# Another written-out order of the steps for a four-layer graph network kernel on one core

## The chip, the core and the metric

The kernel runs on one core of one Trainium2 chip. The metric is the device time of one execution in microseconds, the median of several runs. The core has five engines with a queue of instructions each: TensorE (PE, its weight loads are listed as PEld), VectorE (DVE), ScalarE (ACT), GpSimd (POOL) and SyncE (SP, which here only issues the DMAs of x and of the result).

## The reference, cut to what matters

x has 32 graphs of 512 nodes with 128 features. Every layer takes the layer norm of x, a relu, and adds the layer's result to x. adj is the same 512 by 512 matrix for all graphs.

```python
h = jnp.maximum(_layernorm(x, axis=-1), 0.0)
x = x + _L0_gnn_ref(h, adj, ...)   # attention whose scores come from pairs of nodes, plus h @ self_weight
h = jnp.maximum(_layernorm(x, axis=-1), 0.0)
x = x + _L1_gnn_ref(h, adj, ...)   # graph attention, layer norm, neighbour sum, two-layer MLP
h = jnp.maximum(_layernorm(x, axis=-1), 0.0)
x = x + _L2_gnn_ref(h, adj, ...)   # graph attention, elu
h = jnp.maximum(_layernorm(x, axis=-1), 0.0)
x = x + _L3_gnn_ref(h, adj, ...)   # two projections and one fixed 512 x 512 mixing matrix
```

## The kernel before

The 32 graphs are worked on in 16 groups of two. A group goes through 57 steps (STEPS, lines 50 to 107): `load` reads its x by two DMAs of 256 KB, `store` writes the result back by two such DMAs, and the steps between compute the four layers. Each step has a part on one to three engines. Ten more steps (PREP, "g" in the tables) make the fixed matrix of the last layer once, at the start.

Six groups are in flight, each in a slot of its own: group n uses the tiles whose name ends in n modulo 6 (X4, Y4, HT4 and so on), so group 14 has X2, group 13 X1, group 12 X0, group 11 X5, group 10 X4 and group 15 X3. The x of groups 0 to 2 is read before the main block, that of groups 3 to 5 by `load` once the preparation is over (`edge["done"]`, line 620), since their tiles lie where the preparation's were, and each later one when the group six before it has been stored.

What order each engine works in is written out by hand in TURNS (lines 120 to 139). There is one string for each engine, with one character for each step: the group (0 to f, g for the preparation) whose next step is done. The steps of one group stay in the order of STEPS. HOMES (line 140) says for each PSUM tile, in PE's order, which of the eight PSUM banks it takes. `walk` (line 280) runs through an engine's list and calls a function for each step. Engines wait for each other by semaphores that count the executions of a step. An engine works strictly in its order: a step whose input is late holds up all that stand behind it.

Lines that the steps below touch: `load` waits for the slot's last store and issues its DMAs on SP (lines 616 to 623). `store` waits on SP until DVE has finished the group's last step agg3, then issues two DMAs (lines 625 to 628). `stat0` on DVE takes eight BATCH_NORM_STATS2 of x (line 1154) as soon as x is loaded. `split0` (lines 1211 to 1222) and `low0` (line 1227) on DVE make the operands of `agg0` on PE (line 695); `cmax0` on DVE is lines 1177 to 1189. `mean2` on POOL is lines 1107 and 1109, `top2` on DVE lines 1268 to 1278, and `agg3` on DVE line 1456, twice for a group.

Of the kernel before, what the change touches and what calls it, by code (L numbers as in the profile page):

```python
# [117 lines left out]
    ("eturn", 4, "pe act dve"),  # L118
]
TURNS = {  # L120
    "pe": ("ggggg0110101020g221001241423030413011003310441051152525330125202312322303320414313055000101101040415"
           "2141541504245540525210132132224264222673676643477266237334323443343446764886786648687675785737835778"
           "584838848854595595959965a6a99a56a6a79799696699679675a56656a777787a78776b6ba8bab8a6a7b78aba88b8979b88"
           "abacb8b89cdb9cbadab8cdcd89d9899acaa9ac99daea9cecaacdecebccedbdcdeebd9bddde9e9bebbebceecbeffbfaffbcbd"
           "fcfadafffdffdfcfcccecdcedccfddfeddedffbdeeefeffefebfecedfcffbdcedfefef"),
    "act": ("gg01012g02g10124430301120401310505110301541022130321202303125103301200101411425025443010254524025113"
           "4512345232624246372753644622372343437346446388668747866537573653586877448854788759955956aa9686a69579"
           "876969a67976596559797776a87ba866b6788aba7788b7aa89aba89bc8aa9bbcd9d8aabc8b98d89cab9a99adabaeecc9ccba"
           "edcdbe9cddbb9cedde9bcbeebbcbdcffeaefadcfcbdeadffdfdfccfecfcdecdeffecffddedffbbeedffeeefffbcdccdefdee"
           "ffef"),  # L130
    "dve": ("g012gggg1010g0g2004311120001112254340032110303411041520322051314335522022331330045241143550050101200"
           "2140041154151425153042235041461522372224262672666334467627363772334348534744638677866483846787485788"
           "6735885738849784565799a5959965a99a95866a55799a9a69686779566a596aa77b66778776b7ab7a88a6abbb9bc7a8b8ba"
           "7a898dbba8b8cb88c99daabdcc8d9dc89bca9eaccd9daa99abcecaddce9c9eeedbdceeeddbabd9eac9ecbbefecbdffbffdbb"
           "fbefcffaedcaffffddebccfccefcfdccdfdededffdcdeedffeebeeffeffefcfdcdbefef"),
    "pool": ("01201043210135420135230140521340510201412562374626234767384783865384547989a596a9675a6579ab67687b87bc"
           "ab98da89cad8bcaecd9de9ebc9ebdabfcffeafdcdfcebfdefcdbefdceffe"),
    "sp": ("403502611728394a5b6c7d8e9fdbceaf"),
}
HOMES = ("0123456701235647012356470123564706470647035412670354031254012546073107301254267301570412601326014325"  # L140
         "7601425731432157214536053605367214021402153674053216740532167405321674076405321372164052317641417610"
         "5234763476346347610523476107562347562103471560273145614560273610452736104523764521037036470536476045"
         "3737372163045742574216301567430020432041352670413541326705470540751326074132135607460213574357602143"
         "5760214357602160216243573045106425173064251763401763401767672354016416041604723156407156407123564071"
         "2351235640715236402376415023762736341650345106363276326734514051405140514052673401343526470315246073"
         "1563210745632163074546530742174217465302310231704652657047023165164675012346703546703546172617035426"
         "1703526401735264017351735126402406273514273420674512034672501346725013467251034672467510234670251531"
         "4536702415673567356356735024163574102635741021024635765102437651047365120472047365147365147365120473"
         "6")


def bcast(ap, n):
# [14 lines left out]
def gnn_kernel(nc, x, adj, Wo_d, Ws_d, att0_d, Wp_d, bp_d, asrc_d, adst_d, gatg_d, gatb_d, eps_d, W1_d, b1_d,  # L167
# [12 lines left out]
    with ctx:  # L180
# [62 lines left out]
        tile_at, mat_at, mat_of = {}, {}, []  # L243
        opened, home = [0] * BANKS, iter(HOMES)
        for g, name in order["pe"]:
# [1263 lines left out]
```

How the kernel before makes its waits and increments, by code:

```python
            @block.sync  # L428
            def _(sp):
                for t in range(T):
                    sp.dma_start(adj_raw[:, t, :], adj[t * P:(t + 1) * P, :]).then_inc(adj_loaded, 16)
                for s in range(1):
                    for b in range(G):
                        sp.dma_start(X[s][:, b::G, :],
                                     x.rearrange("b (t p) f -> b p t f", p=P)[s * G + b]).then_inc(x_loaded[s], 16)
                for dst, src in LOADS[0::2]:
                    sp.dma_start(dst, src).then_inc(loaded, 16)
                for s in range(1, NS // 2):
                    for b in range(G):
                        sp.dma_start(X[s][:, b::G, :],
                                     x.rearrange("b (t p) f -> b p t f", p=P)[s * G + b]).then_inc(x_loaded[s], 16)
                for s in taken:
                    sp.sem_inc(s, 1)
                for s in sig["stored"]:
                    sp.sem_inc(s, 16)
                sp.wait_ge(loaded, 16 * len(LOADS[0::2]))
# [1 line left out]
            @block.gpsimd  # L449
# [6 lines left out]
                for bias in (bias_p, bias_1, bias_2):  # L456
                    nc.gpsimd.memset(bias[:].bitcast(F32), 0.0).then_inc(made["pool"], 1)
                pool.wait_ge(made["pool"], 8)
                nc.gpsimd.affine_select(out=ident[:], in_=ident[:], compare_op=ALU.not_equal, fill=1.0, base=0,
# [9 lines left out]
            @block.tensor  # L469
# [9 lines left out]
                mm.then_inc(made["turn"], 1)  # L479
                pe.wait_ge(made["counts"], 1)
                for i in range(T):
```

## Time and profile before

| | us |
|---|---|
| median of 3 runs | 1020.74 (1020.09 to 1025.88) |
| the profiled execution's own time | 1025.88 |
| its span in the profile | 1024.1 |
| PE busy | 957.3 (93%) |
| DVE busy | 870.2 (85%) |
| ACT busy | 632.7 (62%) |
| POOL busy | 549.4 (54%) |
| mean granted clock of TensorE | 0.974 of full speed |

The profiled execution is one of the three timed ones, the longest of them. All times that follow are read in it, in microseconds from the start of its span. The engines' busy times overlap. What an engine waits for is told by the view of the waits, and what stands at a certain time by the timeline.

### The profile page before, as it was taken

What the parts mean: (1) busy time and instruction counts of PE and PEld (TensorE: products, weight loads), DVE (VectorE), ACT (ScalarE), POOL (GpSimd) and SP (SyncE); (2) the same over time, 40 slices, a digit from 0 to 9 for tenths busy, and PEclk for the clock granted to TensorE, in tenths of its full rate; (3) what the DMA queues carried; (4) which work ended last, traced back from release to release, by engine and by line L of the source; (5) the groups of instructions that cost most, each with busy time, mean ns of one, the idle gap of its engine ahead of it and who ended that gap; (6) DMA issues with size and microseconds to landing.
All of it is one profiled execution on the core that took longest, in us unless ns stands there. A gap on an engine that the chain in (4) does not pass through costs nothing. (4 is left out here: it accounts for less than half of the span.)

```text
span 1024.1 us, 21202 instructions
## 1 busy us (share of the span) xinstructions
PE 957.3 (93%) x7355; PEld 908.4 (89%) x7355; DVE 870.2 (85%) x2532; ACT 632.7 (62%) x1641; POOL 549.4 (54%) x1169
## 2 busy tenths in 40 slices
PE   6779999999999999999999999999999899997998
PEld 5679998998988899899989899999899899887897
DVE  5989797999989987978899889699989879779884
ACT  2446557686668653675575674777548584777741
POOL 3426254681786651755566464456727635467831
PEclk9878999999999998999999999999999999999999
DMA  7020000000020010002000101100000100000004
GB/s 141 2 62 2 1 2 1 2 2 1 2 83 2 2 42 2 1 21 63 2 1 1 43 1 42 43 2 22 22 1 2 42 2 2 1 1 2 1 1 124
DMA packets 38490, 20.17 MB, mean 20 GB/s; under 512 B 3184, under 2 KB 37872, under 8 KB 38384
## 3 DMA queue, kind: packets, MB, share of 16 engines
q1 hardware_dynamic: 36512, 18.42, 6.8%
q8 instruction: 59, 0.97, 0.4%
q10 hardware_dynamic: 1872, 0.40, 0.2%
q14 instruction: 47, 0.39, 0.1%
HBM read 10.43 MB, written 8.39 MB: 18 GB/s over the span
## 5 line engine op out<-in xcount | busy, mean ns | idle before, releaser
L639 PE MATMUL ps<-HE,PT 128*128 128x129 f32 x2048 | 241.0, 277 | 5.9 <-issue 2.3
L639 PEld LDWEIGHTS ps<-HE,PT 128*128 128x128 f32 x2048 | 234.8, 193 | 9.3 <-issue 8.6
L925 ACT ACTIVATE Y<-X,SM 128x128 f32<-128x128 f32 x512 | 203.9, 487 | 41.8 <-POOL SM L1083 41.7
L1068 POOL TENSOR_TENSOR SM<-ST 128x8 f32<-128x8 f32 x96 | 28.4, 296 | 294.9 <-DVE ST L1154 294.8
L1291 DVE SCALAR_TENSOR_TENSOR PT<-ps,CE,maskT 128x512 f32<-128x512 f32 x256 | 174.1, 742 | 13.7 <-PE ps L763 7.8
L1079 POOL TENSOR_TENSOR SM<-SM,minus_half 128x8 f32<-128x8 f32 x96 | 162.1, 1688 | 7.6
L639 PE MATMUL ps<-W,HT 128*128 128x128 f32 (+1 forms) x768 | 126.7, 312 | 0.7 <-issue 0.4
L639 PEld LDWEIGHTS ps<-W,HT 128*128 128x128 f32 x768 | 116.0, 193 | 10.1 <-ACT HT L918 0.6
L1154 DVE BATCH_NORM_STATS2 ST<-X 128x6 f32<-128x128 f32 x512 | 104.9, 277 | 3.2
L656 PE MATMUL ps<-ident,Y 128*128 128x128 f32 x640 | 86.5, 279 | 11.5 <-ACT Y L925 9.8
L656 PEld LDWEIGHTS ps<-ident,Y 128*128 128x128 f32 x640 | 72.5, 144 | 17.7 <-ACT Y L925 15.4
L639 PE MATMUL ps<-HI,a_hi 128*128 128x256 f32 x256 | 73.2, 286 | 0.4 <-DVE LOW L1444 0.3
L639 PE MATMUL ps<-HI,a_lo 128*128 128x256 f32 x256 | 72.1, 282 | 0.0
L918 ACT ACTIVATE HT<-ps 128x512 f32<-128x512 f32 x96 | 52.1, 598 | 32.3 <-PE ps L656 32.1
L639 PE MATMUL ps<-LOW,a_hi 128*128 128x256 f32 x256 | 72.0, 281 | 0.0
L959 ACT ACTIVATE HE<-ps,HE 128x128 f32<-128x128 f32 x256 | 69.0, 382 | 0.0
L925 ACT ACTIVATE HE<-Y,SM 128x128 f32<-128x128 f32 x128 | 51.2, 500 | 22.2 <-POOL SM L1083 22.1
L639 PE MATMUL ps<-gin_hi,LOW 128*128 128x512 f32 x128 | 57.7, 451 | 2.1 <-DVE LOW L1310 0.7
L925 ACT ACTIVATE Y<-Y,SM 128x128 f32<-128x128 f32 x128 | 51.0, 491 | 13.4 <-POOL SM L1083 13.4
L1154 DVE BATCH_NORM_STATS2 ST<-Y 128x6 f32<-128x128 f32 x256 | 51.7, 275 | 8.6 <-ACT Y L988 7.8
L1100 POOL TENSOR_TENSOR LOWB<-HE,HIB 128x1024 fp32r<-128x1024 f32 x16 | 35.7, 2228 | 28.5 <-ACT HIB L942 28.5
L639 PE MATMUL ps<-gin_hi,HI 128*128 128x512 f32 x128 | 50.5, 394 | 0.0
(262 smaller groups left out, 2348.9 us busy)
## 6 DMA issues: line engine op xcount, KB each, us to landing
X<-in_x_dram SPq DMA_DIRECT2D x32, 256.0 KB, 3.4
out_dram<-X SPq DMA_DIRECT2D x32, 256.0 KB, 2.8
adj_raw<-in_adj_dram SPq DMA_DIRECT2D x4, 256.0 KB, 3.7
W<-in_L_gnn_W_dram SPq DMA_DIRECT2D x1, 128.0 KB, 5.7
Ws<-n_L_gnn_self_weight_dram ACTq DMA_DIRECT2D x1, 64.0 KB, 3.1
W<-in_L_gnn_W_dram ACTq DMA_DIRECT2D x1, 64.0 KB, 3.5
feat2w<-in_L_gnn_W_dram ACTq DMA_DIRECT2D x1, 64.0 KB, 4.3
Wo<-L_gnn_others_weight_dram SPq DMA_DIRECT2D x1, 64.0 KB, 5.8
```

Source lines behind the costliest of these rows:

```text
L639: return nc.tensor.matmul(o, w, m, start=start, stop=stop, skip_group_check=True)
L656: mm = T_(o[:, t * P:(t + 1) * P], Y[s][:, t * G + b, 0:F], ident[:])
L918: a = A(HT[s][:, b, :], o, ACT.Relu)
L925: a = A(dst[:, n, 0:F], src[:, n, 0:F], func, scale=SM[s][:, S_RSTD, n:n + 1], bias=SM[s][:, S_SHIFT, n:n + 1])
L959: a = A(HE[s][:, k, 0:F], o[:, 2 * P * b:2 * P * b + F], ACT.Identity, scale=HE[s][:, k, F:F + 1])
L1068: TT(sm[:, S_DIF, :], st[:, :, 1], st[:, :, 4], ALU.subtract)
L1079: link(TT(sm[:, S_RSTD, :], sm[:, S_VAR, :], minus_half[:], ALU.pow))
L1100: TT(LOB[s], VA[s], HIB[:].bitcast(F32), ALU.subtract).then_inc(sig["by_pool"][s], 1)
L1154: a = V.bn_stats(ST[s][:, n, :], src(n))
L1291: a = V.scalar_tensor_tensor(out=PT[r][:, j, :], in0=o, scalar=CE[s][:, c:c + 1], in1=maskT[:, j, :].bitcast(F32), op0=ALU.max, op1=ALU.mult)
```

## The change

Only the tables are changed: the strings of TURNS for all five engines and the banks in HOMES. No instruction is added or taken away, and each group's own steps keep their order. Of 470 steps on PE 245 stand at another place in the row, of 404 on ACT 255, of 471 on DVE 260, of 160 on POOL 83 and of 32 on SP 12, nearly all by one to six places.

```diff
     "pool": (
-           "01201043210135420135230140521340510201412562374626234767384783865384547989a596a9675a6579ab67687b87bc"
+           "01201031420153240132453012015430510021421562734626237463748873386584475989a5969a6576a597ab6786787bba"
...
-    "sp": ("403502611728394a5b6c7d8e9fdbceaf"),
+    "sp": ("354100617228394a5b6c7d8e9fedcbaf"),
 }
-HOMES = ("0123456701235647012356470123564706470647035412670354031254012546073107301254267301570412601326014325"
+HOMES = ("0123456701235647012356470356470703570357012364570123016423016420517351357642601357416012760140217634"
...
```

SP at the first loads of the main block. A row is one `load` or `store` of two DMAs, and the number behind X is the slot. Before:

```order
L614 UNCONDITIONAL_BRANCH
L623 DMA X4<-in_x_dram 128x4x128 x2
L623 DMA X3<-in_x_dram 128x4x128 x2
L623 DMA X5<-in_x_dram 128x4x128 x2
L628 DMA out_0_dram<-X0 128x4x128 x2
```

And in the changed kernel:

```order
L614 UNCONDITIONAL_BRANCH
L623 DMA X3<-in_x_dram 128x4x128 x2
L623 DMA X5<-in_x_dram 128x4x128 x2
L623 DMA X4<-in_x_dram 128x4x128 x2
L628 DMA out_0_dram<-X0 128x4x128 x2
```

Group 4's x is now read last of the three instead of first. DVE's own order has stat0 of group 4 and then stat0 of group 3 right behind low0 of group 0 in both kernels.

DVE a little later, from the end of split0 of group 1 (HE1) to the first row of agg0 of group 0 (X0). LOW1 is low0 of group 1, and the five rows with MX2, CF2 and SM2 are cmax0 of group 2. Before:

```order
L1220 TENSOR_TENSOR HE1<-ps0,SM1 128x4x128
L1220 TENSOR_TENSOR HE1<-ps1,SM1 128x4x128
L1227 TENSOR_TENSOR LOW1<-Y1,HI1 128x8x128
L1179 TENSOR_REDUCE MX2<-ps3 128x2
L1184 TENSOR_TENSOR CF2<-CD2,MX2 128x8
L1186 TENSOR_TENSOR SM2<-CD2,MX2 128x4
L1187 TENSOR_TENSOR CF2<-MX2,SM2 128x4
L1188 TENSOR_TENSOR CF2<-CD2,SM2 128x4
L1235 SCALAR_TENSOR_TENSOR X0<-ps3,CE0,X0 128x128 x2
```

And in the changed kernel:

```order
L1220 TENSOR_TENSOR HE1<-ps3,SM1 128x4x128
L1220 TENSOR_TENSOR HE1<-ps2,SM1 128x4x128
L1179 TENSOR_REDUCE MX2<-ps2 128x2
L1184 TENSOR_TENSOR CF2<-CD2,MX2 128x8
L1186 TENSOR_TENSOR SM2<-CD2,MX2 128x4
L1187 TENSOR_TENSOR CF2<-MX2,SM2 128x4
L1188 TENSOR_TENSOR CF2<-CD2,SM2 128x4
L1227 TENSOR_TENSOR LOW1<-Y1,HI1 128x8x128
```

The small cmax0 of group 2 has moved ahead of low0 of group 1, for which PE's agg0 of group 1 waits. PE does self0 of group 0 and then agg0 of group 1 in both kernels.

SP at the end, from the load of the last group, 15 (X3). Before:

```order
L623 DMA X3<-in_x_dram 128x4x128 x2
L628 DMA out_0_dram<-X1 128x4x128 x2
L628 DMA out_0_dram<-X5 128x4x128 x2
L628 DMA out_0_dram<-X0 128x4x128 x2
L628 DMA out_0_dram<-X2 128x4x128 x2
L628 DMA out_0_dram<-X4 128x4x128 x2
L628 DMA out_0_dram<-X3 128x4x128 x2
```

And in the changed kernel:

```order
L623 DMA X3<-in_x_dram 128x4x128 x2
L628 DMA out_0_dram<-X2 128x4x128 x2
L628 DMA out_0_dram<-X1 128x4x128 x2
L628 DMA out_0_dram<-X0 128x4x128 x2
L628 DMA out_0_dram<-X5 128x4x128 x2
L628 DMA out_0_dram<-X4 128x4x128 x2
L628 DMA out_0_dram<-X3 128x4x128 x2
```

The store of group 14 (X2) has moved from the fourth place to the first. The stores of groups 13, 12 and 11 (X1, X0, X5), which stood ahead of it, now stand behind it, and that of group 10 (X4) still does.

## Rows read from the trace of the kernel before

**Rows 1.** The page: span, and busy time of each engine.

```profile
span 1024.1 us, 21202 instructions
PE 957.3 (93%) x7355; PEld 908.4 (89%) x7355; DVE 870.2 (85%) x2532; ACT 632.7 (62%) x1641; POOL 549.4 (54%) x1169
```

**Rows 2.** By stages: us, engines' busy (instructions), granted clock, DMA share, GB/s.

```profile
0.00:49.00 49.00, 34.12 (x147) 29.57 (x148) 36.72 (x121) 15.71 (x30) 18.66 (x45) 0.93 0.37 75
49.00:110.00 61.00, 53.67 (x374) 51.63 (x372) 51.77 (x172) 34.30 (x78) 23.72 (x57) 0.80 0.10 27
110.00:920.00 810.00, 777.65 (x6147) 740.39 (x6147) 704.56 (x2030) 528.19 (x1389) 452.70 (x987) 0.99 0.05 14
920.00:1020.00 100.00, 91.88 (x695) 86.79 (x693) 76.84 (x212) 54.52 (x147) 54.29 (x81) 0.98 0.10 27
```

**Rows 3.** Waits of PE from 110 to 920: total, times, longest.

```profile
PE ps L656 <- ACT Y L925: 5.6, 9, 1.2
...
PE ps L639 <- DVE PT L1291: 2.1, 1, 2.1
```

**Rows 4.** SP's timeline, first loads: start, us, line, tiles; slots 4, 3, 5.

```profile
69.45 0.92 SPq L623 DMA_DIRECT2D X<-in_x_dram  x2
70.48 1.55 SPq L623 DMA_DIRECT2D X<-in_x_dram  x2
72.14 1.14 SPq L623 DMA_DIRECT2D X<-in_x_dram  x2
```

**Rows 5.** DMA issues at 69.86, 70.96 and 72.63: KB, us to landing.

```profile
X<-in_x_dram SPq DMA_DIRECT2D x1, 256.0 KB, 4.4
X<-in_x_dram SPq DMA_DIRECT2D x1, 256.0 KB, 5.1
X<-in_x_dram SPq DMA_DIRECT2D x1, 256.0 KB, 4.9
```

**Rows 6.** DVE's timeline from 74 to 84: stat0 of groups 4, 3; low0; cmax0.

```profile
74.32 3.39 DVE L1154 BATCH_NORM_STATS2 ST<-X 128x6 f32<-128x128 f32 x16
...
81.69 1.23 DVE L1227 TENSOR_TENSOR LOW<-Y,HI 128x1024 fp32r<-128x1024 f32 x1
82.84 0.42 DVE L1179 TENSOR_REDUCE MX<-ps 128x2 f32<-128x256 f32 x1
...
83.71 2.28 DVE L1235 SCALAR_TENSOR_TENSOR X<-ps,CE,X 128x128 f32<-128x128 f32 x8
```

**Rows 7.** PE's timeline: agg0 of group 0, and agg0 of group 1.

```profile
74.46 0.58 PE L639 MATMUL ps<-HI,maskT 128*128 128x256 f32 x1 [2.67 <-DVE LOW L1227]
...
83.22 0.36 PE L639 MATMUL ps<-HI,maskT 128*128 128x256 f32 x1
```

**Rows 8.** By stretches of 5 us: the clock after PE's idle time.

```profile
70.00:75.00 5.00, 1.76 (x12) 1.68 (x13) 4.75 (x13) 2.11 (x2) 0.74 (x1) 0.76 0.88 245
75.00:80.00 5.00, 5.00 (x29) 5.00 (x27) 4.69 (x22) 0.00 (x0) 4.54 (x10) 0.56 0.27 71
```

**Rows 9.** The end: DVE's agg3 of group 14, then stores of groups 14, 15.

```profile
1013.91 0.69 DVE L1456 TENSOR_TENSOR X<-X,ps 128x512 f32<-128x512 f32 x1 [2.16 <-PE ps L639]
...
1014.68 0.92 SPq L628 DMA_DIRECT2D out_dram<-X  x2
...
1020.35 0.92 SPq L628 DMA_DIRECT2D out_dram<-X  x2
```

**Rows 10.** Stores issued at 1014.68 (also 1020.35) and at 1016.24: us to landing.

```profile
out_dram<-X SPq DMA_DIRECT2D x1, 256.0 KB, 2.3
out_dram<-X SPq DMA_DIRECT2D x1, 256.0 KB, 3.5
```

**Rows 11.** The stretch from 1016 to 1019: last numbers are DMA share, GB/s.

```profile
1016.00:1019.00 3.00, 3.00 (x28) 3.00 (x27) 0.69 (x1) 0.00 (x0) 0.00 (x0) 1.00 1.04 288
```

**Rows 12.** DVE's and POOL's timeline: top2 and mean2 of group 11.

```profile
812.10 1.89 POOL L1107 TENSOR_TENSOR HT<-SR,norow 128x1024 f32<-128x1024 f32 x1 [0.96 <-ACT SR L965]
814.07 2.40 POOL L1109 TENSOR_TENSOR HT<-HT,bias 128x1024 f32<-128x1024 f32 x1
812.69 1.33 DVE L1275 TENSOR_TENSOR CF<-DS,MX 128x8 f32<-128x8 f32 x1
813.94 2.56 DVE L1277 TENSOR_SCALAR CF<-DS,MX 128x4 f32<-128x4 f32 x2
```

More of the change, by code:

```diff
@@ L120 @@
 TURNS = {
[L121 to L129, printed above, removed]
-           "ffef"),
[L131 to L135, printed above, removed]
@@ L136 @@
-    "pool": ("01201043210135420135230140521340510201412562374626234767384783865384547989a596a9675a6579ab67687b87bc"
-           "ab98da89cad8bcaecd9de9ebc9ebdabfcffeafdcdfcebfdefcdbefdceffe"),
-    "sp": ("403502611728394a5b6c7d8e9fdbceaf"),
-}
-HOMES = ("0123456701235647012356470123564706470647035412670354031254012546073107301254267301570412601326014325"
[L141 to L149, printed above, removed]
@@ new lines @@
+    "pe": ("ggggg0110102010g212001231424300130411003344100115152255330125202312323230203413134505010000110104114"
+           "1541424525455405025231012122234262422637667643746226377334323346434346768487866446886757578773837785"
+           "8583488488545955959959656a9a9a56a6a7979969669969766a575665a7777878777ab66b8a8ba67aa7bb8aa8bb978b89b8"
+           "ba8cba8bc89dccbdad9cb8a89dd9989caa9aaca9a9e9aacecdcdeccbecedbdcdeeb9dbddde9e9bebbbceecefbfefbffabbcd"
+           "fcfadafffdffdfcfccceccdeddccfdfdeeddffdeebefefffeebfeecdfcffbdcedfefef"),
@@ new lines @@
+    "act": ("gg01102g102g0133244001120031140055110035141021230231203302211303502101001324141055441202550442530214"
+           "1521542332264247632376446227533243467336444838668763678455773635788574684847588957955598a696a66a5897"
+           "9766995a679967655976977778ab86a6b78867ab7a88ba7aa9abb8889bcabca9d8da9bca88bd989cba9a99baaaedecccecab"
+           "9ddbe9ccbdbd9cdeed9bcbeedbcbbcfefafdecfabcdeadfefdfdfccffdccecdeffdecfdfedffbeedfefbeefffbdccdecfdee"
+           "ffef"),
+    "dve": ("g021gggg1010g0g2004311210001112425300431103304101421502352021313355242023132320043113544552005001010"
+           "1140402114455125154330225014612425372224262627666334746662737372334834346673848776364588846477578887"
+           "4637855838894784565799a5998965a999a5566a5a59979966a866795a76695aa77b667787777b6a88ab6aabbb79abbb8aa7"
+           "8cbbd988a8bc8b8c8dd99ccba8add9c89bcaea9c9caa99adabcecdddecc99eeebddceeeddbba9dcea9ecbbfeecdbffbfdffb"
+           "bbefcffadeceffaffddcfcccefcfcdbdcfdceedffdddedeffeebfeefeffefcbfdcefedf"),
@@ new lines @@
+    "pool": ("01201031420153240132453012015430510021421562734626237463748873386584475989a5969a6576a597ab6786787bba"
+           "bc89dac898dbace9dcaed9ebc9ebdafbcffaefdcdfcedfbefdbcefcdeffe"),
+    "sp": ("354100617228394a5b6c7d8e9fedcbaf"),
+}
+HOMES = ("0123456701235647012356470351264703570357012364570123016423016420517351357642601357416012760140217634"
+         "5021756341745613745610261026103745246107361520473604752316047523041675252673041452145214567302121245"
+         "6730125647564301261275304610247530253610253610254734735476102361705243617052417053624627015301530462"
+         "7373715307416256253625037641212156043712456037601260132674501450326732514673067256174253025302536174"
+         "0253617402653165317640235417024170612470613750243750243765176502431424312431765207645207643152076431"
+         "5201576432015671453142607620531453415341762053535203542170617061706106173542062061743506742351674510"
+         "6235106325102563741072456371071030324576176032451763170245631457026270627031456702670236145614561456"
+         "1702345602137604521372137260450645137204561372041563072415630724156307241560371512541603725413760250"
+         "6254137205416451645164564372015620415370642424206153571420635714201642305710571642305716420356420356"
+         "4")
```

## The prediction

> **What bounds the kernel now.** I read the page first. PE is busy for 957.3 of 1024.1 us, DVE for 870.2 [rows 1]: PE is the bound, and a new order, which leaves the work as it is, can only change what PE waits, what clock it gets, and what lies before its first and behind its last instruction. So I cut the span into stages [rows 2]. PE's idle time is 49 - 34.1 = 14.9 us in the preparation, 61 - 53.7 = 7.3 us while the first groups fill the pipeline, 810 - 777.7 = 32.3 us in the long middle, and 100 - 91.9 = 8.1 us while it drains; 4.1 us follow in which only the last result is written. The reader should see that the middle has the most idle time, but spread thin: its costliest kind of wait is nine waits of 5.6 us together, the longest single one 2.1 us [rows 3]. The fill has a mean clock of 0.80 against 0.99 in the middle. The ends of the program have few steps to choose from, so there a moved step can be followed; this is where I look for the terms.
>
> **Term 1, the loads at the start.** Before, SP issues the x of slots 4, 3, 5 in this order [rows 4], and they land, second DMA of each, at 69.86 + 4.4 = 74.3, 70.96 + 5.1 = 76.1 and 72.63 + 4.9 = 77.5 [rows 5]. DVE takes the statistics of group 4 at 74.32, right when its x is there, then those of group 3 [rows 6]. The changed SP order is 3, 5, 4, all held by the same semaphore, so the landing times go to 3, 5, 4. DVE's order still has group 4 first, and DVE works strictly in order: it stands still from 74.3 until 77.5, 3.2 us. Behind it are queued group 3's statistics (already there, no help), coefb0, split0 and low0 of group 1. low0 of group 1 ended at 81.69 + 1.23 = 82.9 [rows 6]; it is now 3.2 us later for the load and 83.71 - 82.84 = 0.9 us later for cmax0 of group 2, which has moved ahead of it, and ends at 87.0. PE started agg0 of group 1 at 83.22, without a wait [rows 7], and stands behind the same steps in both kernels, so it now idles for 87.0 - 83.2 = 3.8 us. This was the cover: before, low0 ended 0.3 us ahead of its use.
>
> How much of this stays? The lower end is 0.5 us: the waits that follow in the fill could each shrink, and 7.3 us of idle time is there in all, though most of it lies before this point. The upper end is 7.2 us: after PE's idle time between 71 and 74.5 (of which 2.67 us is one wait [rows 7]) the clock fell, with a mean of 0.76 and 0.56 in the two stretches of 5 us [rows 8]. At half clock for 2 x (1.2 + 2.2) = 6.8 us, PE lost some 3.4 us of work, and the same could follow a new wait of 3.8 us. I take +3.0: ACT and POOL work ahead meanwhile, and the moved PE steps behind (the transposes of groups 3 and 4 changed places) give back about 1 us.
>
> **Term 2, the stores at the end.** SP is a queue too. Before, the store of group 14 is the fourth of the last six; those of groups 13, 11 and 12 go ahead of it. Now it stands first, and waits for group 14's agg3, which ends at 1013.91 + 0.69 = 1014.6 [rows 9]. Behind it are held the stores of 13, 12, 11 and 10, three of which are ready long before. So ten DMAs of 256 KB instead of four are issued from 1014.68 on, and then the two of group 15. The rate is set by the transfers, not by the issues: 288 GB/s with a DMA share of 1.04 [rows 11], 262,144 bytes in 0.91 us. Check on before: the first DMA lands 2.3 us after 1014.68, at 1017.0, and the fourth at 1016.24 + 3.5 = 1019.7 [rows 10], which is 1017.0 + 3 x 0.91. In the changed kernel the tenth lands at 1017.0 + 9 x 0.91 = 1025.2 and the twelfth at 1027.0. Before, group 15's two landed at 1020.35 + 2.3 + 0.91 = 1023.6. That is +3.4 us, all of it behind the last computation, so nothing hides it. Group 13's agg3 on DVE has moved behind group 14's (1.4 us more), but group 14's transfers cover that. The ends are +2.4 (if the stream runs closer while six stores are queued) and +4.5 (if issues, up to 0.9 us each, gap it).
>
> The page "DMA: Bandwidth & Descriptors" of the Trainium skill (section Specifications) puts the limit of one core's traffic with device memory at about 358 GB/s. By that figure a DMA would take 0.73 us and the term would be 1017.0 + 11 x 0.73 - 1023.6 = +1.4 us. The row has full DMA engines at 288 GB/s, and the sum goes by the row.
>
> **Term 3, the middle.** Half of all steps moved, most by a place or two. Some waits lose their cause. The longest one of the middle, 2.1 us before the attention of group 14 [rows 3], comes from DVE's top2 of group 11: two tiny operations of 8 and 4 columns that took 1.33 and 2.56 us (two instances) while POOL was in mean2 of the same group, and ended when POOL's ended [rows 12]. In the changed kernel POOL does the statistics of group 15 ahead of that mean2 and PE has mlpa1 of group 12 ahead of that attention, so this wait should be gone. Other pairs come closer: on PE, spread2a of group 0 now follows its top2 directly, and norm1 and feat1 of group 0 stand next to each other. Going through PE's neighbours I find as many pairs loosened as tightened, by less than 1.2 us each. I take 0, between -10 and +10, about a third of the 32.3 us of idle time either way. In the drain before 1014 the waits are for chains that DVE's amount of work sets, and DVE does the same amount: 0.
>
> **Sum.** 3.0 + 3.4 + 0 = +6.4 us. The profiled execution took 1025.88 us, so against it the changed kernel comes to 1032.3; it was the longest of three, 5.1 us over the median. Against the median of 1020.74 the forecast is 1027.1, +0.6%. A measurement of this kernel can tell about 1% from no change, so this would most likely read as no change.
>
> **Rivals.**
> A. Tables that lose in the middle as well (slower by over 1%). One mechanism: a new wait of 3.8 us at 83 drops the clock, +3.4 us over term 1's 3.8, and new collisions of top2 with mean2, of the kind above, cost some 2 us of PE each. The page "SBUF — State Buffer" of the Trainium skill (section Who interferes with whom) says that the later one of two such operations waits for the whole of the other, so it takes only a shift of a microsecond to make or lose one. With two collisions: 1020.7 + 3.8 + 3.4 + 3.4 + 4 = 1035.3. For it speaks that the change shuffles hundreds of steps; against it, that the collision I can follow goes away.
> B. The middle gains, not slower than before. The mechanism is the order of PE against its producers: waits like the 9 of 5.6 us for ACT's normalising [rows 3] vanish where more PE work stands between. It outweighs terms 1 and 2 from 6.4 us on, that is if the middle's 32.3 us of idle time fall below 26. If half of them go: 1020.7 + 6.4 - 16.2 = 1011. Against it: I found no side with more loosened pairs.
> C. The change at the start does nothing. PE's later waits absorb all of it and only the stores count: 1020.7 + 3.4 = 1024.1. For it speaks that PE's work, not DVE's, bounds what follows; against it, that PE has hardly a wait to give back between 84 and 110.
>
> **How the numbers follow.** Forecast as summed, 0.45 (1023 to 1031); A, 0.28, all over 1031; C, 0.15; B, 0.12, of which 0.10 is under 1010.5. So faster by over 1% 0.10, slower by over 1% 0.28, within 1% 0.62. The range reaches to B at half of its gain and to a bad A: 1013 to 1039.
>
> **What would show it.** In the profile of the changed kernel: DVE waits about 3 us for a DMA before the statistics at 74; PE waits some 4 us for low0 (line 1227) before agg0 of group 1, at 83; SP issues ten stores in a row from about 10 us before the end on, with 285 GB/s until the end; the time from PE's last instruction to the end grows from 4 to about 7.5 us. PE's idle time from 110 to 920 stays at 32 us, give or take 10. The prediction is wrong if this idle time falls below 20 or rises above 45, or if one of the two terms is absent.

## The result and the profile after

The changed kernel takes 1051.22 us (median of 4 runs, 1049.97 to 1053.9); the kernel before took 1023.31 beside it. The ratio is 1.0276, with a 95% interval of 1.0231 to 1.0322: slower by 2.8%, some 28 us, where +6.4 us was forecast. It lies outside the predicted range. The profiled execution took 1053.7 us, against 1025.88 in that of before, +27.8 us, so the two traces can be set side by side.

The page of the changed kernel, to be held against [rows 1]:

```profile
span 1052.0 us, 21202 instructions
PE 964.9 (92%) x7355; PEld 913.3 (87%) x7355; DVE 873.9 (83%) x2532; ACT 629.9 (60%) x1641; POOL 554.2 (53%) x1169
```

The same instructions, and PE is busy 7.6 us longer with them; the other 20 us are time in which it does nothing. The stages, cut where PE has done the work that it had done at 49, 110, 920 and 1019.4 us before (as near as the orders allow; the first cut is at the same time), columns as in [rows 2]:

```profile
0.00:49.00 49.00, 29.83 (x134) 25.08 (x135) 34.57 (x118) 14.10 (x26) 16.87 (x45) 0.79 0.36 75
49.00:118.50 69.50, 59.62 (x383) 57.25 (x381) 53.61 (x170) 35.29 (x82) 28.90 (x67) 0.75 0.08 24
118.50:944.30 825.80, 783.99 (x6156) 744.71 (x6155) 709.40 (x2037) 526.85 (x1393) 457.81 (x969) 0.99 0.05 14
944.30:1043.70 99.40, 91.41 (x689) 86.26 (x687) 75.64 (x208) 53.67 (x142) 50.67 (x89) 0.98 0.04 12
1043.70:1052.00 8.30, 0.00 (x0) 0.00 (x0) 0.69 (x1) 0.00 (x0) 0.00 (x0) 0.74 0.90 248
```

Read against [rows 2], preparation and fill have grown from 110 to 118.5 us (+8.5), the middle from 810 to 825.8 (+15.8), the drain not at all, and the stretch behind PE's last instruction from 1024.1 - 1019.4 = 4.7 to 8.3 (+3.6). In the middle the idle time of PE rose from 32.3 to 825.8 - 783.99 = 41.8 us (+9.5), and its busy time from 777.65 to 783.99 (+6.3) over the same work. So more than half of the loss is where the prediction put nothing.

What it did follow by hand came as told. SP's first loads come in the new order, and DVE waits for group 4's x with group 3's already there; PE's agg0 of group 1 waits for low0. DVE's and then PE's timeline of the changed kernel, start and duration ahead of each row, the wait in brackets, to be held against [rows 6, 7]:

```profile
80.32 3.19 DVE L1154 BATCH_NORM_STATS2 ST<-X 128x6 f32<-128x128 f32 x16 [3.55 <-DMA X<-in_x_dram]
...
88.41 1.22 DVE L1227 TENSOR_TENSOR LOW<-Y,HI 128x1024 fp32r<-128x1024 f32 x1
```

```profile
89.69 0.58 PE L639 MATMUL ps<-HI,maskT 128*128 128x256 f32 x1 [3.88 <-DVE LOW L1227]
```

3.55 us on DVE (3.2 predicted), 3.88 on PE (3.8 predicted). The clock fell behind it, as after PE's idle time in [rows 8]:

```profile
85.00:90.00 5.00, 1.12 (x9) 0.93 (x8) 4.75 (x12) 3.59 (x7) 3.70 (x5) 0.86 0.01 3
90.00:95.00 5.00, 5.00 (x25) 5.00 (x25) 4.74 (x15) 1.60 (x5) 4.63 (x9) 0.50 0.00 0
```

PE does next to nothing in the first stretch, and in the second, in which it is never idle, a clock of 0.50 was granted: the lower of its two levels.

At the end SP issues all twelve DMAs of six stores in a row, as it had to when group 14's store stands first. SP's timeline, and a stretch of the windows in the stream:

```profile
1038.94 9.63 SPq L628 DMA_DIRECT2D out_dram<-X  x12
```

```profile
1040.00:1044.00 4.00, 3.70 (x32) 3.49 (x30) 1.36 (x3) 0.00 (x0) 0.00 (x0) 1.00 1.02 284
```

The last one lands at 1051.38, 7.7 us behind PE's last instruction (4.1 before; 7.5 predicted). From the first landing, 2.3 us after the first issue as in [rows 10], eleven DMAs take 1051.38 - 1041.24 = 10.1 us, 0.92 each, against 0.91 in the sum. The Trainium skill ("DMA: Bandwidth & Descriptors", Specifications) has 358 GB/s as one core's limit; the trace has 284 with the DMA engines' share at 1.02, so it was right to go by [rows 11].

So the two chains followed came about. The third term, the middle, doesn't hold, and most of the experiments are about it.

### The profile page after: what moved, and what is told of

Its sections match the earlier page's. It is cut to its first block and busy times, and to the rows that moved or that the text cites. A ratio compares the mean times of both kernels' runs of the same rounds, so it can differ in the third digit from the quotient of the medians.

```text
span 1052.0 us, 21202 instructions
## 1 busy us (share of the span) xinstructions
PE 964.9 (92%) x7355; PEld 913.3 (87%) x7355; DVE 873.9 (83%) x2532; ACT 629.9 (60%) x1641; POOL 554.2 (53%) x1169
## 5 line engine op out<-in xcount | busy, mean ns | idle before, releaser
L925 ACT ACTIVATE Y<-X,SM 128x128 f32<-128x128 f32 x512 | 203.9, 490 | 44.8 <-POOL SM L1083 44.8
L1068 POOL TENSOR_TENSOR SM<-ST 128x8 f32<-128x8 f32 x96 | 32.0, 333 | 276.6 <-DVE ST L1154 276.5
L639 PEld LDWEIGHTS ps<-W,HT 128*128 128x128 f32 x768 | 116.1, 194 | 11.2 <-ACT HT L918 2.0
L656 PE MATMUL ps<-ident,Y 128*128 128x128 f32 x640 | 86.2, 280 | 10.1 <-ACT Y L925 8.0
L959 ACT ACTIVATE HE<-ps,HE 128x128 f32<-128x128 f32 x256 | 69.0, 384 | 0.0
L925 ACT ACTIVATE HE<-Y,SM 128x128 f32<-128x128 f32 x128 | 51.1, 500 | 26.9 <-POOL SM L1083 26.9
L925 ACT ACTIVATE Y<-Y,SM 128x128 f32<-128x128 f32 x128 | 51.0, 489 | 13.9 <-POOL SM L1083 13.9
```

Source lines behind the costliest of these rows:

```text
L639: return nc.tensor.matmul(o, w, m, start=start, stop=stop, skip_group_check=True)
L656: mm = T_(o[:, t * P:(t + 1) * P], Y[s][:, t * G + b, 0:F], ident[:])
L925: a = A(dst[:, n, 0:F], src[:, n, 0:F], func, scale=SM[s][:, S_RSTD, n:n + 1], bias=SM[s][:, S_SHIFT, n:n + 1])
L959: a = A(HE[s][:, k, 0:F], o[:, 2 * P * b:2 * P * b + F], ACT.Identity, scale=HE[s][:, k, F:F + 1])
L1068: TT(sm[:, S_DIF, :], st[:, :, 1], st[:, :, 4], ALU.subtract)
```

## The experiments

A few words for what follows. The lag of a kernel is how much later than in the trace of before PE ends the same set of steps, taken where both orders have done the same ones; I worked it out from the two traces by following each step. Each trace is of one execution, so a lag also holds what one execution differs from another: in five traces whose order up to 113 us is the old one it stands between -2.2 and 2.2 us there. "Ends undone" is the changed kernel with the loads at the start and the stores at the end in the old order. Each ratio is to the kernel before, measured beside it on the same chip.

| kernel | us | ratio | interval |
|---|---|---|---|
| changed kernel | 1051.22 | 1.0276 | 1.0231 to 1.0322 |
| its loads as before | 1048.15 | 1.0222 | 1.0185 to 1.0259 |
| its stores as before, DVE's order left | 1052.71 | 1.0284 | 1.0254 to 1.0315 |
| before with SP's new order alone | 1031.31 | 1.0069 | 1.0044 to 1.0094 |
| ends undone | 1043.66 | 1.0184 | 1.0148 to 1.022 |
| before to 135 us, then changed | 1050.98 | 1.0256 | 1.021 to 1.0302 |
| changed to 145 us, then before | 1035.0 | 1.01 | 1.0055 to 1.0146 |
| before to 596 us, then changed | 1036.24 | 1.0109 | 1.007 to 1.0149 |
| changed to 615 us, then before | 1043.99 | 1.0192 | 1.0153 to 1.0231 |
| before with POOL's new order alone | 1104.47 | 1.0808 | 1.076 to 1.0856 |
| ends undone, mean2 of group 1 earlier | 1042.05 | 1.0179 | 1.0137 to 1.0221 |
| before without mean2 | 1022.66 | 0.9999 | 0.998 to 1.0018 |
| ends undone without mean2 | 1034.55 | 1.0127 | 1.0092 to 1.0162 |
| before, new order from 358 to 466 us | 1025.06 | 0.9999 | 0.9975 to 1.0023 |
| before, new order from 135 to 353 us | 1033.93 | 1.0084 | 1.0049 to 1.0118 |

**The loads.** The changed kernel, SP's string with the old start.

```diff
-    "sp": ("354100617228394a5b6c7d8e9fedcbaf"),
+    "sp": ("403502611728394a5b6c7d8e9fedcbaf"),
```

> The changed kernel (1051.2 us, against 1023.3 before) with SP's first loads in the old order (slots 4, 3, 5); the stores at the end stay changed. Theory F (the fill's loss comes from the late x of group 4): DVE's wait of 3.5 us and PE's wait of 3.9 us before agg0 of group 1 go, PE's wait shrinks to below 1 us, and with the half clock that followed it the time falls by 4 to 8 us, to 1043 to 1047. Rival D (DVE and PE are late anyway in the new fill, the load only fills a hole): the time falls by less than 2 us.

DVE's wait of 3.55 us is down to 0.41, PE's of 3.88 to 0.84, and the ratio falls by 0.54% of 1024, 5.5 us, with an uncertainty of 6 (the medians themselves differ by 3.1). The chain is shown, its size isn't told by this pair.

The traces tell more. From 78 to 113 us of before, the stretch around this wait, PE falls back by 5.2 to 5.8 us in the four traces that have the new order with the new loads, and gains 0.2 to 1.4 us in the four that have the new order with the old loads. So in the changed kernel's own fill the late load costs some 6.5 us, not 3: 3 us of waiting, and behind it 17.0 us of PE at the lower clock from 85 us on where the run of this section has 6.8.

**The stores, by SP alone.** The same kernel with the old end of SP's string instead.

```diff
-    "sp": ("354100617228394a5b6c7d8e9fedcbaf"),
+    "sp": ("354100617228394a5b6c7d8e9fdbceaf"),
```

> The changed kernel with SP's last stores in the old order (groups 13, 11, 12, 14, 10, 15); the loads stay changed. Theory S (ten stores queued behind group 14's set the end): the time between PE's last matmul and the end falls from 8.3 to some 4.7 us, and the whole time by 3.4 to 3.8 us, to 1047.5. Rival: the end is set by DVE's moved agg3 of group 13, and less than 1 us is won.

A miss: nothing is gained. Group 13's store is first again, but on DVE group 13's agg3 still stands behind group 14's, so the row of twelve can't start earlier: it starts 3.1 us before PE's last instruction, in the changed kernel 4.7, and its last landing is 9.3 us behind that instruction instead of 7.7. SP's timeline, then DVE's (the second half of agg3 of group 14, agg3 of group 13, the first half of that of 15):

```profile
1037.32 9.65 SPq L628 DMA_DIRECT2D out_dram<-X  x12
```

```profile
1034.90 0.69 DVE L1456 TENSOR_TENSOR X<-X,ps 128x512 f32<-128x512 f32 x1 [2.16 <-PE ps L639]
1035.83 1.41 DVE L1456 TENSOR_TENSOR X<-X,ps 128x512 f32<-128x512 f32 x2 [0.24 <-DVE X L1456]
1037.73 0.69 DVE L1456 TENSOR_TENSOR X<-X,ps 128x512 f32<-128x512 f32 x1 [0.49 <-PE ps L639]
```

The prediction saw DVE's swap and said that the stream covers it. That is so in the changed kernel, and it is also why this half-undoing does nothing: one queue's order can't be put back without the order of what it waits for.

**Both of SP's changes alone.** The kernel before, one line changed.

```diff
-    "sp": ("403502611728394a5b6c7d8e9fdbceaf"),
+    "sp": ("354100617228394a5b6c7d8e9fedcbaf"),
```

> The kernel before with nothing changed but SP's string, which is the changed kernel's: loads 3, 5, 4 first, and the store of group 14 first of the last six. Both theories of the prediction on the old tables. Theory F and S: DVE waits some 3.4 us for the x of group 4 and PE idles about 3 us at agg0 of group 1, of which 1 to 3 us last; from PE's last matmul to the last landing 7.7 us instead of 4.1; in sum 5 to 7 us over before. Rival (the old fill has the slack to take the late load): 3.6 us over before, all of it at the end.

+7.1 us on 1023.5, interval 4.5 to 9.6, for terms 1 and 2 on the old tables; their sum was +6.4. DVE and PE in its trace:

```profile
76.95 2.23 DVE L1154 BATCH_NORM_STATS2 ST<-X 128x6 f32<-128x128 f32 x11 [3.20 <-DMA X<-in_x_dram]
```

```profile
85.47 0.58 PE L639 MATMUL ps<-HI,maskT 128*128 128x256 f32 x1 [3.14 <-DVE LOW L1227]
```

The wait on DVE is the predicted 3.2 us to the digit; PE's is 3.14 (without the moved cmax0, which is DVE's string). The last landing is 7.7 us behind PE's end. From 78 to 113 us PE falls back by 1.2 us in this trace and gains 0.1 to 3.4 us in five others with the old order there: 1.3 to 4.6 us for the load, less than in the changed kernel.

**Both ends undone.** Now the changed kernel with all of SP's string as before, and DVE's agg3 of groups 13 and 14 in the old order.

```diff
-    "sp": ("354100617228394a5b6c7d8e9fedcbaf"),
+    "sp": ("403502611728394a5b6c7d8e9fdbceaf"),
...
     "dve": (
...
-           "bbefcffadeceffaffddcfcccefcfcdbdcfdceedffdddedeffeebfeefeffefcbfdcefedf"),
+           "bbefcffadeceffaffddcfcccefcfcdbdcfdceedffdddedeffeebfeefeffefcbfdcefdef"),
```

> The changed kernel with SP's whole string of before, and DVE's agg3 of group 13 ahead of group 14's again. The run with the stores alone in the old order won nothing, since the store of group 13, first again, waited for an agg3 that DVE now does behind group 14's. Theory S2 (store order and agg3 order belong together): from PE's last matmul to the last landing 4.1 us instead of 7.7, and with the loads' 3.0 us the time is 1051.2 - 3.6 - 3.0 = 1044.6. Rival (the end costs nothing in the median): 1048, as with the loads alone.

The last landing is 4.1 us behind PE again, and 1.0184 stays: +18.8 us (15.1 to 22.5) with neither of the two terms in it. The difference to the changed kernel, 1.0276 - 1.0184, is 9.4 us with an uncertainty of 6, in line with 7.1 from SP's string alone and with 6.5 + 3.6 from the traces. So the failed step is the middle's 0. The two traces show 14.4 us of the 18.8: the profiled execution of this kernel was the fastest of its four (1040.31), that of the kernel before the slowest of its three. Its stages, 108.5 and 932.7 being the cuts for before's 110 and 920:

```profile
49.00:108.50 59.50, 51.99 (x374) 49.58 (x372) 52.00 (x168) 34.41 (x80) 31.23 (x67) 0.83 0.10 28
108.50:932.70 824.20, 782.84 (x6157) 743.42 (x6157) 709.17 (x2038) 527.67 (x1394) 458.98 (x969) 0.99 0.05 14
```

The fill is as quick as before, the middle is 824.2 instead of 810 us: +9.0 idle, +5.2 busy.

**Is it the start after all, or a place?** Four splices: each engine does in one order the steps that it had started by a certain time in that order's own trace, and the rest in the other order. The strings of POOL show how little that moves, first 135/145 us, then 596/615 us (the first row of each pair is the kernel before):

```diff
-           "01201043210135420135230140521340510201412562374626234767384783865384547989a596a9675a6579ab67687b87bc"
+           "01201031420153240135230140521340510201412562374626234767384783865384547989a596a9675a6579ab67687b87bc"
...
-           "01201043210135420135230140521340510201412562374626234767384783865384547989a596a9675a6579ab67687b87bc"
+           "01201043210135420135230140521340510201412562374626234767384783865384547989a596a9675a6579ab6768787bba"
```

> Spliced tables: all that the kernel before had started until 135 us (the first 51 steps of PE, with their banks, and SP's first loads), then the changed kernel's order for all the rest, stores too. Theory P (time is lost where it shows in the comparison of the two traces: 7.5 us until here, the rest after): 1051.2 - 7.5 = 1043 to 1045. Rival C (all that follows is a consequence of the worse fill, whose delay DVE hands on): the time falls to that of before plus the stores' 3.6 us, 1027.

> The opposite splice: all that the changed kernel had started until 145 us, then the order of the kernel before for the rest, with its stores. Theory P: 1023.3 + 7.5 = 1030 to 1032. Rival C (the fill alone makes the later loss): 1047, the changed kernel's time less the stores' 3.6 us.

> Spliced: all that the kernel before had started until 596 us, then the changed order. Theory P (a lag arises where the order of that stretch makes it): between this place and PE's end the changed kernel loses 5 us more, and 3.6 us at the stores: 1023.5 + 8.6 = 1032. Rival C (lag depends on the whole history): nearer to 1045.

> The opposite splice: the changed order until 615 us, then that of the kernel before with its stores. Theory P: the changed kernel's lag at this place, 17 us without the 2 us that its profiled start was late, stays constant to the end: 1040. Rival C: the old order takes the lag back in part, 1030 or less.

With the old order up to 135 us, so without the new start, 1.0256 of 1.0276 is left: the middle's loss is no echo of the start's. With the new order up to 145 us only, the lag is 9.4 us at 158 us and still 9.1 at 470; it then goes up to 12.4 in three steps, each beside a stretch at the lower clock in one of the two traces: the old order behind the seam wins nothing back. The same with 615 us: 16.5 us at the seam, 16.2 at 653, 16.2 at 932, 15.8 at the end. And the new order from 596 us on costs 11.2 us, of which 3.9 are the stores (landing 8.0 us behind PE). So there is no single place. Both halves of the middle lose. Rival C falls in all four. In size theory P is missed too: the times are 3 to 8 us above what it gave. And the start alone and all the rest, 10.2 + 26.2 us, make more than the whole change (28.2), at the edge of the intervals. The splices say where time is lost; they don't price it to a few us.

**One engine's order alone.** Of the single engines, POOL's order is one that can be put into the kernel before without a circle of waits.

```diff
-           "01201043210135420135230140521340510201412562374626234767384783865384547989a596a9675a6579ab67687b87bc"
+           "01201031420153240132453012015430510021421562734626237463748873386584475989a5969a6576a597ab6786787bba"
...
```

> The kernel before with the order of ONE engine changed: POOL's string is the changed kernel's; PE, ACT, DVE, SP and the homes are as before. Theory (the middle's loss is made by the orders of PE, ACT, DVE and POOL together, by small waits where a step of one engine stands behind a step of another that is no longer early): POOL alone is idle more than half of the span, so its order costs little: ratio 1.000 to 1.005 (0 to +5 us). Rival (POOL's order is what loses, since its ops now run beside DVE's top2 and lock it out): most of the +18.8 us of the run with both ends undone comes with it, ratio 1.010 or more.

The theory misses, and what happened is not the rival either, though its "1.010 or more" is met: +82 us, more than four times the 18.8, from the engine that is idle for almost half of the span. PE's waits for ACT's L925 alone come to 50.8 us in its trace, and those shown next go back to POOL's waiting, not to a collision. The first large piece, POOL's, ACT's and PE's timelines:

```profile
203.22 0.21 POOL L1068 TENSOR_TENSOR SM<-ST 128x8 f32<-128x8 f32 x1 [11.97 <-DVE ST L1154]
```

```profile
212.90 3.18 ACT L925 ACTIVATE Y<-X,SM 128x128 f32<-128x128 f32 x8 [10.97 <-POOL SM L1083]
```

```profile
216.14 1.97 PE L656 MATMUL ps<-ident,Y 128*128 128x128 f32 x8 [6.41 <-ACT Y L925]
```

POOL stands at gats1 of group 2 (the statistics in the middle of the second layer), whose input DVE, still in the old order, has ready only at 203.1. In POOL's new row stat2 of group 0 comes behind it instead of ahead of it, though DVE had its input done at 198.0. ACT's normalising of group 0 waits for that, and PE for ACT. A row for one engine holds only together with the others' rows. It also shows how steep this is: moves by a few places on the least used of the four computing engines cost PE 6 us at one place, and 12 us of an in-order engine's waiting hide in a row that reads harmlessly.

**One of the new waits by itself.** In the trace with both ends undone the longest new wait of PE is 2.54 us before spread2a of group 1. The collision of [rows 12] has turned up for another group. POOL's, DVE's and PE's timelines:

```profile
230.82 1.90 POOL L1107 TENSOR_TENSOR HT<-SR,norow 128x1024 f32<-128x1024 f32 x1
232.80 2.34 POOL L1109 TENSOR_TENSOR HT<-HT,bias 128x1024 f32<-128x1024 f32 x1
```

```profile
231.17 1.57 DVE L1275 TENSOR_TENSOR CF<-DS,MX 128x8 f32<-128x8 f32 x1
232.66 2.50 DVE L1277 TENSOR_SCALAR CF<-DS,MX 128x4 f32<-128x4 f32 x2
...
235.46 0.61 DVE L1340 SCALAR_TENSOR_TENSOR Y<-ps,SM,HT 128x128 f32<-128x128 f32 x2
...
236.37 0.61 DVE L1340 SCALAR_TENSOR_TENSOR Y<-ps,SM,HT 128x128 f32<-128x128 f32 x2
```

```profile
236.22 0.62 PE L763 MATMUL ps<-ident,CE 128*128 128x128 f32 x4 [2.54 <-DVE Y L1340]
```

Two operations of 8 and 4 columns end when POOL's two of 1024 columns end, 4 us for what takes 0.6 us alone. Behind them in DVE's row stands elu2b of group 0 (L1340), which empties the bank that PE needs next. That is bank 2 by the new HOMES; by the old ones spread2a of group 1 takes bank 1, which ACT's norm1 of group 4 leaves. So the new banks have a part in this wait beside the new rows. Before, this top2 ran at 223.8, mean2 at 227.4. The test moves mean2 of group 1 on POOL one place forward, ahead of stat1 of group 5:

```diff
-           "01201031420153240132453012015430510021421562734626237463748873386584475989a5969a6576a597ab6786787bba"
+           "01201031420153240132453012015430150021421562734626237463748873386584475989a5969a6576a597ab6786787bba"
```

> The changed kernel with both ends undone, and on POOL the step mean2 of group 1 put ahead of stat1 of group 5 (before it stood behind it, and ran 230.8 to 235.1 beside DVE's top2 of group 1, 230.7 to 235.2, which takes 0.9 us alone; PE then waited 2.54 us for bank 2, and half-clock work followed). Theory (the wait comes from the collision): top2 of group 1 takes about 1 us, PE's wait before spread2a of group 1 goes, the lag behind the kernel before at 262 us falls from 7.1 to 3 to 4.5 us; of the whole time 1 to 4 us, so a ratio of 1.014 to 1.018 against 1.0184. Rival (the loss is only moved: the next thing that is late takes its place): the lag at 262 stays at 6 to 8 us, ratio 1.017 to 1.020. Whole-time difference is at the edge of what the rounds tell; the lag in the trace decides.

DVE's timeline at the same step, then PE's:

```profile
231.60 0.18 DVE L1275 TENSOR_TENSOR CF<-DS,MX 128x8 f32<-128x8 f32 x1
231.70 0.41 DVE L1277 TENSOR_SCALAR CF<-DS,MX 128x4 f32<-128x4 f32 x2
```

```profile
233.95 1.10 PE L763 MATMUL ps<-ident,CE 128*128 128x128 f32 x8
```

Collision and wait are gone, and the lag at 262 us is 4.5 us instead of 7.1: about what the wait of 2.54 us cost is won. In the whole time 1.0179 against 1.0184 can't be told apart, as was to be feared from 2.6 us. The local cause is shown; it is one of many. In the changed kernel a stretch at the lower clock followed the same wait. The trace with both ends undone has none there, against what the expectation says. The changed kernel's windows:

```profile
240.00:245.00 5.00, 3.33 (x31) 3.09 (x29) 4.80 (x7) 2.09 (x7) 4.60 (x4) 1.00 0.01 2
245.00:250.00 5.00, 4.16 (x24) 3.99 (x25) 4.23 (x11) 5.00 (x17) 0.00 (x0) 0.66 0.00 0
```

**All collisions with mean2.** In both the kernel before and the one with both ends undone, mean2's two POOL operations are cut to 8 elements (the attention's mean base is left out of the computation).

```diff
-                    link(TT(m, repeat(SR[s][:].rearrange("p b f -> p (b f)"), T), bcast(norow[:], G * F), ALU.mult))
+                    link(TT(m[:, 0:1, 0:8], repeat(SR[s][:].rearrange("p b f -> p (b f)"), T)[:, 0:1, 0:8],
+                            bcast(norow[:], G * F)[:, 0:1, 0:8], ALU.mult))
...
-                    TT(m, m, repeat(bias2[:], TG), ALU.add).then_inc(sig["by_pool"][s], 1)
+                    TT(m[:, 0:1, 0:8], m[:, 0:1, 0:8], repeat(bias2[:], TG)[:, 0:1, 0:8],
+                       ALU.add).then_inc(sig["by_pool"][s], 1)
```

> The kernel before, its two POOL operations of mean2 cut from 64-column rows of all groups to 8 elements of one (the attention's mean base is left out, so those values are not the reference's). It takes away 16 times 4 us of POOL and all its collisions with DVE's top2. For the pair with the next run. Theory (collisions with mean2 are a small part of the difference): this is 0 to 4 us faster than the kernel before, ratio 0.996 to 1.000, and the next run stays 12 to 18 us behind this one. Rival (rival A of the prediction, collisions make the middle's loss): this one gains little, the next gains 8 us or more on it.

> The changed kernel with both ends undone, and mean2's two POOL operations cut in the same way (same part left out). Theory: ratio to the kernel before 1.010 to 1.017, that is 12 to 18 us behind the run before this one. Rival (collisions of top2 with mean2 make the middle's loss): ratio 1.006 or less, within 8 us of the run before this one.

The old order gains nothing, the new one some 6 us (1.0184 to 1.0127, with an uncertainty of 5), and 13 of its 19 us stay. Collisions with mean2 are a part of the loss, about a third by these medians and not surely a small one; 13 us are there without them. A count in the traces speaks against more collisions as the cause: taking together all DVE operations that run over 0.4 us longer than the same form usually does, they lose 20.6 us in the kernel before and 21.7 with both ends undone. The new order has hardly more of them; what differs is what stands behind them. (With mean2 cut 6.2 and 12.7 us are left, mostly beside other long operations of POOL, so this pair doesn't take all collisions away.) The Trainium skill's rule ("SBUF — State Buffer", Who interferes with whom), that one of two such operations waits for the whole of the other, fits the collisions shown here (DVE's 1.57 and 2.50 us end when POOL's two end), but as the explanation of the 19 us it isn't enough.

**One stretch alone, twice.** The kernel before with the new order from 135.3 to 353 us only, and from 358 to 466 us only (POOL's row shown, in this order):

```diff
-           "01201043210135420135230140521340510201412562374626234767384783865384547989a596a9675a6579ab67687b87bc"
+           "01201043210135420132453012015430510021421562734626237467384783865384547989a596a9675a6579ab67687b87bc"
...
-           "01201043210135420135230140521340510201412562374626234767384783865384547989a596a9675a6579ab67687b87bc"
+           "01201043210135420135230140521340510201412562374626234763748873386584475989a596a9675a6579ab67687b87bc"
```

> The same for the stretch before it: old order until 135.3 us, the changed kernel's until 372 us of its own time (about 106 of PE's steps), old order for the rest; start and stores old. With both ends undone the lag rose from about 0 to 9.1 us over these steps. Theory (the stretch makes its loss by itself): ratio 1.006 to 1.010 (6 to 10 us slower), the lag made by 353 us and flat behind it. Rival (the lag needs the new fill ahead of it, or is made up for by what stands behind): ratio 1.000 to 1.004, or a lag that falls again behind 353 us.

> The kernel before with the changed order in one stretch only: each engine does the steps that it started before 358 us in the old order, then those that the changed kernel started by 480 us in the new one (about 50 of PE's 470), then the rest in the old one; start and stores are old. In three traces with the new order the lag behind the kernel before FALLS in this stretch (from 9.1 to 4.2 us, from 4.8 to -1.9, from 5.7 to 0.6), of which about 3 us are half-clock work of the trace of before near 386 us. Theory (a stretch's order makes its own gain or loss, whatever stands around it): a ratio of 0.995 to 0.999 (1 to 5 us faster), and the lag in the trace falls by 2 to 5 us between 358 and 466 us. Rival (the new order only made up there a delay that the old order doesn't have, since DVE and ACT had run ahead of a PE that was late): ratio 1.000 to 1.004.

The first stretch costs 8.6 us by itself, as expected. The windows of before and of this kernel over the same 1675 instructions of PE, then over all that follow:

```profile
135.00:353.00 218.00, 211.22 (x1675) 200.51 (x1674) 194.64 (x559) 154.61 (x395) 135.22 (x292) 1.00 0.04 11
353.00:1019.40 666.40, 634.46 (x4954) 603.09 (x4954) 563.64 (x1620) 415.47 (x1097) 363.29 (x750) 0.98 0.06 18
```

```profile
137.00:365.00 228.00, 213.52 (x1675) 203.48 (x1675) 194.08 (x559) 153.80 (x396) 138.31 (x301) 0.99 0.04 11
365.00:1030.40 665.40, 633.03 (x4958) 601.64 (x4956) 565.93 (x1621) 415.95 (x1096) 363.78 (x743) 0.99 0.06 18
```

228 for 218 us, idle time 14.5 for 6.8, busy time +2.3; and 665.4 for 666.4 behind it. That the lag isn't quite flat there (12.4 us at 353, 9.4 at 465, 10.9 at 577 and 11.0 at the end) comes with half-clock work, which the trace of before has at 386 us and this one elsewhere. What PE waits for in that stretch, first in the kernel before (135 to 353 us), then here:

```profile
PE ps L639 <- issue: 1.7, 3, 1.2
PE ps L763 <- ACT CE L948: 1.2, 3, 0.5
PE ps L656 <- ACT Y L925: 1.1, 1, 1.1
PE ps L639 <- DVE X L1235: 0.8, 2, 0.6
```

```profile
PE ps L763 <- DVE Y L1340: 2.8, 2, 2.6
PE ps L754 <- DVE MX L1265: 2.4, 3, 0.9
PE ps L639 <- DVE X L1235: 2.1, 1, 2.1
PE ps L639 <- DVE LOW L1227: 1.7, 1, 1.7
PE ps L656 <- ACT Y L925: 1.6, 2, 1.1
PE ps L763 <- ACT CE L948: 1.5, 1, 1.5
```

The old order's longest wait is 1.2 us; the new one has five from 1.1 to 2.6, and DVE ends three of these. DVE does the same work, with another group's step ahead of the one that PE needs. The 1.7 us before agg0 of group 3, for instance: PE has done the same steps before it in both orders, but DVE's row has turned from agg0 of group 2, gat1 of group 0, low0 of group 3 to gat1, agg0, low0, and stands still 3.0 us before gat1, with low0 behind it.

The second stretch, in which three traces with the new order win 5 to 7 us on before, wins nothing under the old order: 0.9999. The expectation's 1 to 5 us are not seen (the interval is -2.6 to +2.3 us). About 3 us of that gain was half-clock work that the trace of before happens to have at 386 us. At the seam a new wait of 3.74 us of PE for ACT's L959 stands against the rest, so the stretch by itself may still gain a little. A kernel faster than both is not shown, and no other run here points to one.

## Why the prediction was wrong

**Term 1, the loads: right in its chain, too small in what stays.** Wait of DVE 3.55 and of PE 3.88 us against 3.2 and 3.8. What stays of it was taken as +3.0. On the old tables that holds: both terms together measured 7.1 (4.5 to 9.6) with SP's string alone, and the stores take 3.6 of it, so 3.5 are left. In the changed kernel the traces have some 6.5 us, near the upper end of 7.2, which was the wait of 3.8 and 3.4 for the clock behind it. The 1 us that the moved steps of PE were to give back is not seen. The preparation of the changed kernel's profiled execution also began late (lag 2.0 us at 36 us, where nothing was moved that matters), part of the +8.5 us up to 118.5 that is no cost of the change: with both ends undone the same stretch was 1.5 us shorter than before.

**Term 2, the stores: right.** +3.6 against +3.4, by the mechanism and the rate told.

**Term 3, the middle: this step failed.** It reads: "Going through PE's neighbours I find as many pairs loosened as tightened, by less than 1.2 us each. I take 0, between -10 and +10". The runs have +18.8 us in its place (with both ends undone), 8.6 in the stretch 135 to 353 us tried alone, and 7.3 from 596 us on, the stores taken off. Three things in the step were wrong.

First, neighbours on PE tell half of it. A wait of PE is made on the producer's engine as well, by what stands ahead of the needed step there: elu2b of group 0 behind a stretched top2, low0 of group 3 behind a waiting gat1 or, with POOL's row alone, stat2 of group 0 behind another group's gats1. Before the waits of 1.7 and 2.1 us (agg0 of group 3, gin1 of group 0) PE's neighbours are the same in both orders. And "by less than 1.2 us each" was too small: before spread2a of group 1 feat1 of group 4, 2.5 us of PE, has moved from ahead of it to behind it, just the cover that the 2.54 us lack.

Second, gains and losses aren't alike. Between the kernel before and the one with both ends undone, step by step from PE's first step of the preparation on, 26.4 us of PE's idle time went and 36.2 came. The waits that went could be looked at beforehand (the 2.1 us before group 14's attention is down to 0.17, as told). Of the 36.2 that came, 27.5 stand before steps that had waited for nothing, and the waits of the trace of before can't name those. That an order whose longest wait is 1.2 us over 218 us leaves a shuffle more places to lose than to win is my reading of it; one new order doesn't show it for others.

Third, the bound of +10 counted idle time alone. It was met: 32.3 became 41.8 us, and by the test in the prediction ("wrong if above 45") the term would have passed. But 6.3 us of busy time came on top (5.2 with both ends undone), for which the term had nothing. The lower clock is only a part of that. By the granted clock in the traces the middle has 17.1 us at the lower level before, 23.9 in the changed kernel and 20.5 with both ends undone. At half the clock 6.8 us more cost at most 3.4 of the 6.3, and 3.4 us more at most 1.7 of the 5.2. Nor is that share shown to belong to the new order, for the trace with SP's string alone has 20.5 us in the old middle too. And the trace with mean2 of group 1 earlier has only 6.8 us, less than before, and PE still ends 8.2 us later. So the new order loses without the clock's help; what the rest of the busy time is stays open.

**The rivals.** A, slower by over 1% with new waits, clock and collisions, is nearest to what happened: its +3.4 us for the clock in the fill is there. But the loss is twice that of its 1035.3, and its collisions are the smaller part. Against it was held that the one collision that I could follow goes away; it does, and another comes. B, a middle that gains, fell; C, a start that does nothing, fell too.

What stays open: the 3 us or so between the sum of the stretches tried (8.6 + 0 + 7.3) and 18.8, which is within the intervals, and the stretch from 466 to 596 us, which wasn't tried alone. Open too is the share of the banks. HOMES changed together with the rows, no run changes it alone, and in the 2.54 us wait followed above the new bank has a part. Of the many small waits only that one was taken away by a run.

## What to carry to other kernels

An order written out for five in-order engines is one object: look for the step that stands ahead of the needed one on the producer's engine, not for neighbours on the consumer, and expect that one engine's row alone can be far worse than either whole order (POOL's: +8%). Where the bounding engine of the kernel before waits little and briefly, expect a loss and not a zero from a shuffle without a named wait to remove. Price a wait of several us with its length and the clock behind it (3.9 us in the fill came to some 6.5), and leave room for work that gets slower for no reason that you can name. The waits of a chain that can be followed step by step (a load, a queue of stores) can be predicted to the half microsecond, what stays of them in the fill can't; give the part that can't be followed a range of the size of all small waits it could make, with its middle on the losing side.

## What had not been expected of the hardware

A delay made in one stretch stays, under an order in which every engine has idle time: 9.4 us to within 0.3 over 310 us, 16.2 to within 0.1 over 280, 10.9 to within 0.1 over 440 but for two places (9.3 near 830, 12.3 near 947), at which the two traces have their stretches of lower clock at different times; all of it moves as one. Executions of one kernel differ by more than the change of one wait does: the four executions of the kernel with mean2 of group 1 earlier span 1034.05 to 1042.71, at mean clocks of 0.983 to 0.962, the slower with the lower. Removing 16 times 4 us of POOL's work from the kernel before gave 0.9999 (0.998 to 1.0018): none of POOL's work taken away there was in PE's way.
